# Layer 3's mixture of experts: tokens sorted by expert through DRAM instead of every token through every expert

## The reference

```
gates = softmax(xt @ gate_w)                      # E = 8 experts
top_v, top_i = top_k(gates, K)                    # K = 2
top_v = top_v / sum(top_v)
h  = gelu(einsum('nd,edf->enf', xt, fc_w))        # 128 -> 512, each expert
eo = einsum('enf,efd->end', h, proj_w)            # 512 -> 128
out = sum(eo[top_i] * top_v)                      # two experts of a token
```

## Time and profile before

| | us |
|---|---|
| the profiled execution's own time | 1490.01 |
| its span, first to last instruction | 1488.2 |
| median of three executions | 1489.48 |
| TensorE busy | 1388.7 (93%) |
| VectorE busy | 776.7 (52%) |
| ScalarE busy | 746.8 (50%) |
| GpSimd busy | 142.5 (10%) |
| DMA | 27.88 MB, mean 19 GB/s |

### The profile page before, as it was taken

How to read it: one execution, slowest core, us unless ns; L and a number is a source line. 1 busy time by engine, 2 the same in 40 slices (tenths; PEclk the granted TensorE clock), 3 DMA queues, 4 the chain that set the end, 5 groups by cost and what they waited for, 6 DMA issues and landing times.

```text
span 1488.2 us, 26260 instructions
## 1 busy us (share of the span) xinstructions
PE 1388.7 (93%) x8852; PEld 1133.2 (76%) x8852; DVE 776.7 (52%) x2083; ACT 746.8 (50%) x1526; POOL 142.5 (10%) x131
## 2 busy tenths in 40 slices
PE   6898999999999988999978899999999998898998
PEld 5686577777998766879947866777789887577898
DVE  4784544554434746643256835445544456475532
ACT  3763455555543454444447635555555435544543
POOL 1054000000000001000011610000000100020000
PEclk9999999999999999989989999999999999999999
DMA  5002000000002000000000020000000020000000
GB/s 206 1 1 114 0 1 1 1 1 2 1 1 81 33 1 1 6 1 12 5 17 1 1 114 1 1 1 1 1 1 1 2 114 2 1 1 1 1 8 8
DMA packets 4038, 27.88 MB, mean 19 GB/s; under 512 B 1054, under 2 KB 1344, under 8 KB 2880
## 3 DMA queue, kind: packets, MB, share of 16 engines
q1 hardware_dynamic: 3184, 22.55, 3.9%
q10 hardware_dynamic: 720, 3.59, 0.6%
HBM read 25.09 MB, written 1.05 MB: 18 GB/s over the span
## 4 chain that ended last, share of the span: by engine, by line
issue 61%; PE 26%; POOL 5%; DVE 4%; ACT 2%; DMA 1%; SPq 0%; DVEq 0%; POOLq 0%; ACTq 0%
PE psum L663 24%; PE psum L697 3%; POOL probs L1270 2%; POOL rs L1224 1%; DMA moe<-in_w_folds_dram 1%; POOL arenaD L1239 1%; POOL probs L1264 1%; DVE arenaA L1597 1%; DVE xn L1330 0%; POOL x L1251 0%; DVE arenaA L1595 0%; ACT seen L1009 0%; DVE stat L1306 0%; ACT arenaB L1009 0%; DVE hn L1348 0%
## 5 line engine op out<-in xcount | busy, mean ns | idle before, releaser
L663 PEld LDWEIGHTS psum<-moe,arenaA 128*128 128x128 f32 x2048 | 239.5, 194 | 8.3 <-issue 1.9
L663 PE MATMUL psum<-moe,arenaA 128*128 128x128 f32 x2048 | 241.9, 278 | 2.2 <-DVE gt L1479 1.4
L1009 ACT ACTIVATE arenaB<-psum 128x512 f32<-128x512 f32 x448 | 167.8, 426 | 109.4 <-PE psum L697 108.0
L1009 ACT ACTIVATE arenaA<-psum,vec 128x512 f32<-128x512 f32 (+1 forms) x208 | 125.4, 614 | 164.3 <-PE psum L663 163.9
L663 PE MATMUL psum<-arenaD,arenaB 128*128 128x128 f32 (+2 forms) x1440 | 188.0, 279 | 8.0 <-ACT arenaB L1009 7.3
L663 PEld LDWEIGHTS psum<-arenaD,arenaB 128*128 128x128 f32 (+1 forms) x1440 | 173.4, 193 | 18.2 <-issue 10.7
L1427 DVE SCALAR_TENSOR_TENSOR x<-psum,gt,x 128x128 f32<-128x128 f32 x256 | 72.1, 344 | 214.0 <-PE psum L663 214.0
L1009 ACT ACTIVATE probs<-probs,nmax 128x589 f32<-128x589 f32 x128 | 100.7, 787 | 164.4 <-DVEq L1453 164.2
L1450 DVE CUSTOM_DVE_ANT_0 probs<-psum,shift 128x589 f32<-128x589 f32 x128 | 98.7, 771 | 149.9 <-PE psum L663 148.6
L697 PE MATMUL psum<-w_first,probs 128*128 128x128 f32 (+2 forms) x1120 | 161.3, 275 | 12.0 <-POOL probs L1270 6.9
L663 PE MATMUL psum<-parts 128*128 128x512 f32 x672 | 166.4, 398 | 0.0
(11 more groups left out here) (203 smaller groups left out, 1797.4 us busy)
## 6 DMA issues: line engine op xcount, KB each, us to landing
moe<-in_w_moe_dram SPq DMA_DIRECT2D x4, 4096.0 KB, 12.9
moe<-in_w_folds_dram SPq DMA_DIRECT2D x3, 1024.0 KB, 10.2
w_l<-in_w_l_dram ACTq DMA_DIRECT2D x1, 1372.0 KB, 12.8
x<-in_x_dram SPq DMA_DIRECT2D x4, 256.0 KB, 3.9
out_dram<-x SPq DMA_DIRECT2D x4, 256.0 KB, 2.1
w_rest<-in_w_rest_dram ACTq DMA_DIRECT2D x1, 768.0 KB, 9.0
w_first<-in_w_first_dram ACTq DMA_DIRECT2D x1, 596.0 KB, 5.4
w_second<-in_w_second_dram ACTq DMA_DIRECT2D x1, 512.0 KB, 6.7
```

Source lines behind the costliest of these rows:

```text
L663: return nc.tensor.matmul(out, lhsT, rhs, start=start, stop=stop, skip_group_check=shared)
L1009: return nc.scalar.activation(out, in_, func, **kw)
```

## The change

Part 3 is no longer dense. For each sequence the 1024 (token, expert) choices are put in order of experts, and each expert's rows are rounded up to tiles of 128. Two choices for each of 512 tokens and 8 experts fill at most 8 + 7 = 15 tiles, so there are always 15 tiles a sequence, 30 a pair.

- `places` (TensorE, VectorE): 8 small products count, for each token and choice, how many stand before it; some 20 small operations of VectorE make from it a row number for each choice (`row_at`, 2 x 4 columns of 128) and the expert of each tile (`expert_at`).
- `rows_out` (POOL): 8 indirect transfers write the normed tokens, 128 rows of 512 bytes each, to their places in a DRAM buffer. SP reads the buffer back in two transfers (`load_rows`, tiles 0 to 4 and 5 to 14) when all eight have landed.
- For each tile SP reads the tile's expert from `expert_at` into a register (`value_load`) and loads that expert's 512 KB of weights into one of 8 buffers in `moe`. Load n waits until tile n - 8 is through TensorE. The weights in DRAM are laid out so that an expert's part is 4 KB a partition.
- For each tile TensorE does `row_turn` (one transposition), `row_hidden` (4 products with 128 columns), `row_out` (4 products); ScalarE copies the transposed tile and applies Gelu; VectorE copies the result. In step m of the new list they stand for tiles m, m - 1 and m - 2.
- SP sends the results in groups of five tiles to DRAM (`send_rows`). `rows_back` (POOL): 8 indirect transfers gather the two rows of each token. `combine` (VectorE): 8 operations add them to x, weighted.
- Both splits, and the transfer of 4 MB, are gone for part 3. The products of part 3 are now all in plain 32-bit floats.
- Sequence 0's `places` and `rows_out` stand in unit 50 of part 2. Sequence 1's choice is made between the tiles: norm in steps 2 to 4, logits and `gates` in 5 to 7, `places` and `rows_out` in 7; its first tile is 15. `rows_back(0)` is in step 18, `combine(0)` and the next norm in 24, the transpose for part 4 in 27. `rows_back(1)` is in unit 1 of `small_attention(4)`, `combine(1)` in unit 4, the norm, transpose and projections of sequence 1 in units 4 to 7 (2 to 6 before).
- Before the loop, both DRAM buffers for rows are cleared from a zeroed tile.

```diff
@@ schedule
+    def rows_step(m):
+        if m < len(ROWS3):
+            do("row_turn", *ROWS3[m], m, wide())
+        if 1 <= m <= len(ROWS3):
+            do("row_hidden", *ROWS3[m - 1], m - 1, wide())
+        if m >= 2:
+            do("row_out", *ROWS3[m - 2], m - 2, gen())
...
+        if k == half + 18:
+            do("places", 0, spare(k))
+            do("rows_out", 0)
...
-        if n < k < n + 5:
-            hidden(3, 0, (k - n - 1) // 2, *((0, 1), (2, 3))[(k - n - 1) % 2])
+        if n + 2 <= k < n + 4:
+            rows_step(k - n - 2)
...
-    moe(3, 0, choosing(3, 1))
-    moe(3, 1, {0: (lambda: norm_stats(4, 0), lambda: do("sum_columns", 0), lambda: do("sum_columns", 1)),
-               1: (lambda: norm_apply(4, 0),), 3: (lambda: norm_turn(4, 0),),
-               4: (lambda: do("project_heads", 4, 0, gen(), turn(), turn(), big()),)})
+    between = {2: (lambda: norm_stats(3, 1),), 3: (lambda: norm_apply(3, 1),), 4: (lambda: norm_turn(3, 1),),
+               5: (lambda: do("logits", 3, 1, gen()), lambda: gates(3, 1, 0)), 6: (lambda: gates(3, 1, 1),),
+               7: (lambda: gates(3, 1, 2), lambda: do("places", 1, gen()), lambda: do("rows_out", 1)),
+               18: (lambda: do("rows_back", 0),), 20: (lambda: do("sum_columns", 0), lambda: do("sum_columns", 1)),
+               24: (lambda: do("combine", 0), lambda: norm_stats(4, 0)), 25: (lambda: norm_apply(4, 0),),
+               27: (lambda: norm_turn(4, 0),),
+               30: (lambda: do("project_heads", 4, 0, gen(), turn(), turn(), big()),)}
+    for m in range(2, len(ROWS3) + 2):
+        rows_step(m)
+        for step in between.get(m, ()):
+            step()
...
+    small_attention(4, {1: (lambda: do("rows_back", 1),), 4: (lambda: do("combine", 1), lambda: norm_stats(4, 1)),
+                        5: (lambda: norm_apply(4, 1),), 6: (lambda: norm_turn(4, 1),),
+                        7: (lambda: do("project_heads", 4, 1, gen(), gen(), turn(), big()),),
@@ SyncE
+            def load_rows(s):
+                sp.wait_ge(scattered[s].sem, it[0] * 128 + 128)
+                for h, (a, b) in enumerate(((0, 5), (5, TILES3))):
+                    sp.dma_start(xg[s][:, 128 * a:128 * b].rearrange("p (j d) -> p j d", d=128),
+                                 dram[f"rows{s}"][128 * a:128 * b, :].rearrange("(j p) d -> p j d", p=128)).then_inc(rows_in[s][h].sem, 16)
...
+                for n, (s, j) in enumerate(ROWS3):
+                    if j == 0:
+                        sp.wait_ge(*placed.at(s))
+                    if n >= NB3:
+                        sp.wait_ge(*tensor_did("ro", n - NB3))
+                    expert = sp.value_load(expert_at[0:1, s, j:j + 1], min_val=0, max_val=E - 1)
+                    sp.dma_start(moe_rows[n % NB3], dram["w_moe1"][:, bass.ds(expert * 1024, 1024)]).then_inc(weights_in[n % NB3].sem, 16)
+                    if n in (NB3 - 1, 17):
+                        load_rows(int(n == 17))
+                    if n >= NB3 and (n - NB3) % GROUP3 == GROUP3 - 1:
+                        send_rows((n - NB3) // GROUP3)
+                send_rows(4)
+                send_rows(5)
@@ GpSimd
+            def rows_out(s):
+                pool.wait_ge(*placed.at(s))
+                pool.wait_ge(cleared.sem, 16 * NS)
+                pool.sem_inc(held_pool.sem, 1)
+                for n in range(2 * NT):
+                    nc.gpsimd.indirect_dma_start(dram[f"rows{s}"], bass.IndirectOffsetOnAxis(ap=row_at[:, s, n:n + 1], axis=0),
+                                                 xn[:, s, n % NT, :], None).then_inc(scattered[s].sem, 16)
+            def rows_back(s):
+                for g in range(3 * s, 3 * s + 3):
+                    pool.wait_ge(*group_sent(g))
+                pool.sem_inc(held_pool.sem, 1)
+                for n in range(2 * NT):
+                    nc.gpsimd.indirect_dma_start(back[s][:, 128 * n:128 * n + 128], None, dram[f"outs{s}"],
+                                                 bass.IndirectOffsetOnAxis(ap=row_at[:, s, n:n + 1], axis=0)).then_inc(gathered[s].sem, 16)
@@ VectorE
+            def combine(s):
+                dve.wait_ge(gathered[s].sem, it[0] * 128 + 128)
+                for n in range(2 * NT):
+                    ins = v.scalar_tensor_tensor(x[:, s, n % NT, :], back[s][:, 128 * n:128 * n + 128], plc[:, s, 48 + n:49 + n],
+                                                 x[:, s, n % NT, :], ALU.mult, ALU.add)
```

More of the change, by code:

```diff
@@ L91 @@
 TILES0 = [(s, k) for s in range(NS) for k in (4, 0, 1, 2, 3)]
+TILES3 = L * 2 // 128 + E - 1
+ROWS3 = [(s, j) for s in range(NS) for j in range(TILES3)]
+NB3, GROUP3 = 8, 5
 def in_parts(l, s, e):
-    return l in (3, 7) and (s, e) not in ((0, 0), (0, 1))
-PARTED = [(l, s, e) for l in (3, 7) for s in range(2) for e in range(E) if in_parts(l, s, e)]
+    return l == 7 and (s, e) not in ((0, 0), (0, 1))
+PARTED = [(l, s, e) for l in (7,) for s in range(2) for e in range(E) if in_parts(l, s, e)]
 class Rotor:
@@ L544, in program @@
         gate_exp = signal("gate_exp")
+        chosen_ready = signal("chosen_ready")
+        placed = signal("placed")
+        held_pool = signal("held_pool")
+        cleared = signal("cleared")
+        scattered = [signal(f"scattered_{s}") for s in range(NS)]
+        rows_in = [[signal(f"rows_in_{s}_{h}") for h in range(2)] for s in range(NS)]
+        weights_in = [signal(f"weights_in_{b}") for b in range(NB3)]
+        rows_sent = [signal(f"rows_sent_{h}") for h in range(2)]
+        gathered = [signal(f"gathered_{s}") for s in range(NS)]
         high_part = signal("high_part")
@@ L639, in _ @@
             load_x(1, 0)
+            sp.wait_ge(consts_ready.sem, 6)
+            for s in range(NS):
+                sp.dma_start(dram[f"rows{s}"].rearrange("(p j) d -> p (j d)", p=128), arenaB[:, 0:128 * TILES3]).then_inc(cleared.sem, 16)
             with sp.Fori(0, PAIRS - 1) as pair:
@@ L913, in logits, with places, row_turn, row_hidden @@
                 last.then_inc(*filled[i].mark("logits", l, s))
+            def places(s, i):
+                need(pe, "earlier")
+                pe.wait_ge(*chosen_ready.at(s))
+                take(i)
+                chosen = gt[:, s, 6, :]
+                mm(slot(i, NT * E), W["earlier"], chosen, stop=False, shared=True)
+                for t in range(NT):
+                    c = chosen[:, E * t:E * t + E]
+                    if t < NT - 1:
+                        mm(slot(i, E * (NT - 1 - t), at=E * (t + 1)).rearrange("p (r e) -> p r e", e=E), W["ones"],
+                           c.unsqueeze(1).broadcast_to([128, NT - 1 - t, E]), start=False, stop=t == NT - 2, shared=True)
+                for t in range(NT):
+                    last = mm(slot(i, E, at=NT * E), W["ones"], chosen[:, E * t:E * t + E], start=False, stop=t == NT - 1, shared=True)
+                last.then_inc(*filled[i].mark("pl", s))
+            def row_turn(s, j, n, i):
+                pe.wait_ge(rows_in[s][int(j >= 5)].sem, it[0] * 16 + 16)
+                take(i)
+                tr(slot(i, 128), xg[s][:, 128 * j:128 * j + 128], 128).then_inc(*filled[i].mark("rt", n))
+            def row_hidden(s, j, n, i):
+                pe.wait_ge(*weights_there(n))
+                read(i, "rt", n)
+                take(i)
+                for f in range(FT):
+                    last = mm(slot(i, 128, at=128 * f), moe_rows[n % NB3][:, 128 * f:128 * f + 128], xgT[n % 2])
+                last.then_inc(*filled[i].mark("rh", n))
+            def row_out(s, j, n, i):
+                read(i, "rh", n)
+                take(i)
+                for f in range(FT):
+                    last = mm(slot(i, 128), hid3[n % 2][:, 128 * f:128 * f + 128],
+                              moe_rows[n % NB3][:, 512 + 128 * f:640 + 128 * f], start=f == 0, stop=f == FT - 1)
+                last.then_inc(*filled[i].mark("ro", n))
             def turn_gates(s, i):
@@ new lines, in row_out @@
+            def row_out(s, j, n, i):
+                g = n // GROUP3
+                if n % GROUP3 == 0 and g >= 2:
+                    dve.wait_ge(*group_sent(g - 2))
+                dve.wait_ge(*filled[i].at("ro", n))
+                a = 128 * (n % (2 * GROUP3))
+                v.tensor_copy(sent_rows[:, a:a + 128], slot(i, 128)).then_inc(*free[i].mark("ro", n))
+            def combine(s):
[3 more added lines that the diff above has]
+                                                 x[:, s, n % NT, :], ALU.mult, ALU.add)
+                    if n % NT == NT - 1:
+                        link(ins)
@@ L1610, in _ @@
                          logits=logits, gates=gates, turn_gates=turn_gates, gate_bias=gate_bias,
+                         places=places, row_out=row_out, combine=combine,
                          project_heads=project_heads, global_net=global_net, couple=couple)
@@ L1744 @@
         "b1_3": col(a["L3_ffn_b1"]), "g": same(gates),
```

(4 more changed lines are left out.)

90 lines of the change are left out of this document (79 added, 11 removed).

## The result

Four executions of the changed kernel took 1464.16, 1465.39, 1472.69 and 1475.73 us, with a median of 1469.04; the kernel before, on the same chip, has 1488.39. The ratio is 0.9864, interval 0.9836 to 0.9892: 1.4% faster. The sign holds, and so does the wide range of 1412 to 1494, but the gain is 19 us by the medians, not 46, and 1469 lies outside the forecast's own range of 1427 to 1462. The profiled execution is the fastest of the four: 1464.16 us, span 1462.3, which is 25.8 under the one before.

What follows compares the result with a forecast made beforehand. Part 3 was taken as bound by TensorE alone: 43.4 us gained less 19.3 lost is 24.1 a pair, 48 for both, so 1490.0 becomes 1442 us (chance 0.52, own range 1427 to 1462; wide range 1412 to 1494).

Steps and rivals of the forecast that it cites:

- TensorE: work removed less work added: Part 3, per pair: 102.3 us of products go, 55.7 of tiles and 3.2 for places and logits come; gain 43.4.
- hand-off 1: Sequence 0 sorted at part 2's end: 1.2 us lost to VectorE's small operations, 1.0 to short tile steps.
- hand-off 2: Sequence 1 sorted between part 3's tiles: 1.0 us lost waiting for its choice, TensorE stands 6.3 us at tile 15.
- hand-off 3: Sequence 0's results gathered during part 3: combine(0) barely in time, 1.2 us lost before the transposition in step 27.
- hand-off 4: Sequence 1's results gathered at part 4's start: VectorE 3.8 us late at combine(1), plus combine's 2.75: 6.6 us lost.
- clock: Two TensorE stands of 4 to 6 us a pair lower the granted clock: about 2 us more lost per pair.
- c: Price of one indirect transfer on POOL in part 3's new path, taken as 1.2 us.
- rival (d): POOL itself is the bound: at 3 us per indirect transfer, 21 us a pair slower, 1532 us; chance 0.10.
- rival (a): Hand-offs nearly free, 0.33 us per indirect transfer: 36.3 us gained a pair, 1417 us; chance 0.13.
- Rival (b): The eight indirect transfers don't overlap, each takes a 2.1 us landing: 1.4 us gained a pair, 1487 us; chance 0.13.
- Rival (c): SP's loop bounds part 3, 3 us a tile instead of 1.0: 12 us a pair, 1466 us; chance 0.12.
- u: Moment in part 3 when sequence 1's scatters have landed; sequence 0's gathers were forecast complete 22.4 us after it.

Runs made afterwards that it cites:

- experiment 2: Against the changed kernel, each tile's weight load brings 64 KB instead of 512 KB, all else as before: 1459.59 us, ratio 0.9778.
- experiment 4: Against the changed kernel, result groups 0 to 4 are sent from ScalarE's queue instead of SP's: 1468.41 us, ratio 0.9851.
- experiment 7: Against the changed kernel, SP sends group 1 before waiting for sequence 1's scatters and reads its tiles 5 to 14 back later: 1468.81 us, ratio 0.9855.
- experiment 5: Against the changed kernel, only list places moved: combine(0) from step 24 to 26, combine(1) from unit 4 to 6, following norm steps and projections later: 1440.99 us, ratio 0.9677.
- experiment 8: Against the changed kernel, only each token's first row is gathered, 4 indirect transfers a sequence and 4 adds instead of 8: 1447.32 us, ratio 0.9726.
- experiment 6: Against the changed kernel, TensorE makes 40 filler transpositions before waiting for tile 15's rows: 1464.16 us, ratio 0.9825.
- experiment 9: Against the changed kernel, the later combines (step 26, unit 6) and 40 filler transpositions before tile 15's rows together: 1438.92 us, ratio 0.9656.
- experiment 1: Against the changed kernel, both combines read a constant tile and the wait for the gathers stands in part 5; transfers stay: 1444.51 us, ratio 0.9698.
- experiment 11: Against the changed kernel, only combine(1) moved to unit 6, its apply, transposition and projections to unit 7: 1457.54 us, ratio 0.9785.

## Why the forecast had the sign and not the size

The ledger of one pair, in us; measured in pair 1 of the profiled execution.

| term | forecast | measured |
|---|---|---|
| TensorE: work removed less work added | 43.4 | 42.0 |
| hand-off 1 (sequence 0 sorted in part 2) | 2.2 | 0.6 |
| hand-off 2: wait for `places`, stand at tile 15 | 1.0 + 6.3 | 1.3 + 5.3 |
| hand-off 3: sequence 0 back | 1.2 | 6.5 + 1.1 |
| hand-off 4: sequence 1 back | 6.6 | 9.7 |
| clock | 2.0 | 6.8 |
| left | 24.1 | 10.7 |

From the tokens' transposition for part 3 (304.68 before, 306.33 after) to the same step for part 5 (521.49, 513.49) the pair gained 9.65 us, so the ledger is closed to 1.1 us. Most of that is in how stands are read: a record of 8 products lasts 1.06 us where the next ones start after 0.89, so each stand between two records is some 0.17 us too short, and four of the terms are such stands. The 1.1 beside hand-off 3 is part 4's first product, which waits 1.05 us for VectorE's work on the queries (453.99) and had no wait before.

**TensorE's sum, right.** 30 tiles at 1.90 instead of 1.86 are 1.2 more, `places` 1.7 instead of 1.6 a sequence.

**POOL's price, right.** One transfer behind the other is 393.32 to 400.89 in six steps, 1.26 us, where c = 1.2 was taken; rival (d) needed 2.15, and rival (a) 0.33. Rival (b) falls: the eight scatters have landed 11.2 us after the first one's start (391.98 to 403.14, when SP goes on), and eight landings of 2.1 would be 16.8. The 17.2 us that the prediction worked out from the Trainium skill's fit ("DMA: Bandwidth & Descriptors", "Anatomy of one DMA — SWDGE (gpsimd) path") for eight transfers without overlap fall with it. That fit is for one transfer, 2.15 us for 64 KB: the last scatter, 2.25 us from its issue to its landing (400.89 to 403.14), is near it, and the last gather is not, 3.8 us (467.24 to 471.00) beside part 7's load.

**Hand-offs 1 and 2, right in kind, 1.6 and 0.7 us less than forecast.** The stretch of part 2 between two fixed points grew from 56.26 to 58.14 us, 1.88, of which `places` itself is 1.7; one wait of 0.4 follows. The 4.2 us of small operations on VectorE, for which 1.2 was taken, are hidden. Tile 15's rows came 3.6 us after the scatters (4.6 forecast).

**Rival (c), wrong.** Where they wait for nothing, loads leave SP 1.0 to 1.5 us apart, not 3, and no tile of pair 1 waited for weights.

**Hand-off 3: the step that failed.** "`combine(0)` is due after step 24, at u + 23.2: in time, barely" came from gathers complete at u + 22.4. With u = 403.1 the store was issued at u + 10.3 (8.3 forecast), had landed at u + 17.2 (10.7), and the gathers were complete at u + 31.5 (22.4): 9 us late, 6.8 of which VectorE stood at `combine`. The sends and gathers were priced by the row of a quiet store, 2.1 us, and SP's loads only by the time to issue them. But between u and the send SP puts 0.98 MB of rows, 2.62 MB of weights and 0.66 MB of results into the transfer engines, 4.3 MB, and these moved 323 GB/s (last column of the first row below): 13 us of work in line. Experiments 2, 4 and 7 show that it is these bytes and no queue: 64 KB loads bring the landing to 2.8 and end the stand; another queue or order leaves it at 6. The same traffic holds the last gathers, which took 434.58 - 430.01 = 4.6 us to land, and 1.8 in experiment 2.

**Hand-off 4, mechanism right, size off.** The forecast had `combine(1)` reached at 10.6 and the rows at 14.4 after the last product. VectorE got there at 9.2 and the rows at 18.2 (last product's end at about 452.8): it stood 9.0 us instead of 3.8. From part 4's first product to part 5's transposition it is 59.5 us instead of 47.5, 12.0 more, of which 2.3 are the clock's (below). Of the 3.8 us that the rows are later, 1.7 is the last tile's copy, which stood behind `project_heads(0)` on VectorE, 1.2 the store (458.39 - 454.74 = 3.6 us to POOL's first gather, 2.4 forecast), 0.7 the landing of the last gather (2.8 after its issue ended, 2.1 forecast) and 0.2 the gathers' issues. The prediction counted "copy, issue and landing" as if nothing were queued before the copy. Experiment 5 took that away too. And it put nothing for the weights of part 7, which "come when part 3 is over, as before": now eight gathers are in the transfer engines with these 4 MB. In the changed kernel POOL's issues take most of that time, so 0.7 us is what can be seen; in experiment 8, with half the issues, the last gather lands 7.8 us after its issue, at the same time as the 4 MB. No run moved this load, so what it costs in all stays open.

**Clock, too small.** Three stretches of the changed kernel, the loaded one of hand-off 3 and those behind the second and third stand:
```profile
410.25:430.00 19.75, 19.75 (x180) 19.75 (x179) 2.91 (x10) 9.02 (x21) 7.58 (x8) 1.00 0.95 323
...
440.00:453.99 13.99, 12.75 (x86) 11.34 (x84) 5.03 (x16) 4.12 (x7) 2.27 (x1) 0.85 0.08 23
...
477.00:485.00 8.00, 7.85 (x43) 7.19 (x44) 4.95 (x13) 2.95 (x7) 0.00 (x0) 0.71 0.00 0
```
The first tile after the stand at tile 15 cost 3.54 us for 1.90, 1.6 lost; after the second stand the first step lost 1.2, and 14 us at 0.85 another 2.1 (0.15 x 14), of which 0.4 lies in the first step and is in the 1.2 already; after the third, 8 us at 0.71 lost 2.3. That is 6.8 against 2.0. It is TensorE's work at the 1.2 GHz level behind these three stands, and experiment 6 shows one of the losses go when the stand is filled. A shorter stand can have it too: behind 2.59 us in experiment 9 (435.76) eight products took 1.84 us instead of 1.06. And taking a stand away does not always bring the clock back, since in experiment 1 the mean stayed at 0.964.

**Where the gain went.** A late gather costs nothing until an engine that works in order stands in front of it. Moving a few steps in the list recovered 28 us, all that was missing against the forecast; removing the waits instead, 24.5 (experiment 1). That the forecast's number was met by experiment 5 does not make its ledger right: there it is smaller stands on both ways back, beside a clock term larger than forecast. The weak point could be seen in the working: a margin of 0.8 us on a sum with three landings that no row of a loaded stage had priced. The store's and the gather's 2.1 us at twice their size would have made the 1.2 a 4.6 (1.2 + 4.2 - 0.8). The signs that the prediction named for being wrong could not show this: tiles 2 us apart or a wait of 14 us at tile 15 did not come, and the time was missed all the same.

## What to carry to other kernels

A wait on an in-order engine should be placed by the late bound of what it waits for, not by its mean: here the later places, with the last tile's copy no longer behind other work, gave 28 us for no change in work or transfers. How much each of the moved steps gives was not run apart, beyond experiment 11. Price a DMA landing by the bytes issued before it on all queues, since the landing of a store in a quiet stage (2.1 us) was a third of that in a loaded one (6.0). Look for old transfers that a new one now meets, such as part 7's weights here. And look at what stands before the last small copy that starts a chain of transfers.

## What the runs showed of the hardware

An indirect transfer of 128 rows of 512 bytes holds POOL 0.95 us, with 0.30 us to the next one, scatter and gather alike. The last of eight scatters had landed 1.3 us after its issue ended (401.85 to 403.14), less than the 2.1 us taken for it. The last of eight gathers took 4.6 us among 512 KB loads, 1.8 among 64 KB ones, and 2.8 at the end of a load of 4 MB. Beside that load a gather took 6.2 us from issue to landing, by the median of eight. A store of 320 KB landed in 2.7 us in quiet engines and 6.0 among 512 KB loads (6.8 until POOL went on). Reading a register from SBUF and issuing one load took SP 1.0 to 1.5 us together, where SP waited for nothing.
